# Cross-attention and a quantised feed-forward block on one core: the opening order of all five engines written anew

## The reference, cut to what matters

```
x = x + xattn(layernorm(x), ctx)      # q = x Wq, k = ctx Wk, v = ctx Wv, 8 heads of 64, softmax, Wo, bo
x = x + ffn(layernorm(x))
ffn(x) = bitlinear(silu(bitlinear(x, w_gate)) * bitlinear(x, w_up), w_down)
bitlinear(x, w) = act_quant(x) @ weight_quant(w).T
weight_quant(w): s = 1 / mean(|w|); round(w * s) clipped to -1..1, over s
act_quant(x):    s = 127 / max(|x|) per row; round(x * s), over s
```

## Time and profile before

| | before |
|---|---|
| median of 3 runs (lowest, highest) | 1103.38 us (1101.78, 1104.1) |
| profiled execution: span from first to last instruction | 1103.9 us |
| PE busy | 1079.8 us, 98% |
| DVE busy | 965.3 us, 87% |
| ACT busy | 742.6 us, 67% |
| POOL busy | 501.5 us, 45% |

### The profile page before, as it was taken

How to read it: one execution, slowest core, us unless ns; L and a number is a source line. 1 busy time by engine, 2 the same in 40 slices (tenths; PEclk the granted TensorE clock), 3 DMA queues, 4 the chain that set the end, 5 groups by cost and what they waited for, 6 DMA issues and landing times.

```text
span 1103.9 us, 17477 instructions
## 1 busy us (share of the span) xinstructions
PE 1079.8 (98%) x5528; PEld 496.4 (45%) x5528; DVE 965.3 (87%) x2081; ACT 742.6 (67%) x947; POOL 501.5 (45%) x645
## 2 busy tenths in 40 slices
PE   8879999999999999999999999999999999999998
PEld 6434444444444444444444444444444444444443
DVE  5997898998889988888989988888899889988985
ACT  3997767757656667777665677777666656666543
POOL 0255554565445454554444446555543444344111
PEclk9998999999999999999999999999999999999999
DMA  9997665353555635544564553655455555554334
GB/s 352 281 241 149 117 125 114 82 116 87 110 124 122 123 86 106 118 88 106 121 123 91 109 115 91 106 116 114 98 105 119 119 107 104 106 110 96 72 77 100
DMA packets 355963, 133.80 MB, mean 121 GB/s; under 512 B 332448, under 2 KB 332960, under 8 KB 355360
## 3 DMA queue, kind: packets, MB, share of 16 engines
q1 hardware_dynamic: 355872, 132.70, 54.4%
HBM read 34.08 MB, written 16.78 MB: 46 GB/s over the span
## 4 chain that ended last, share of the span: by engine, by line
PE 78%; DVE 7%; ACT 2%; issue 1%; DMA 1%; POOL 0%; SPq 0%; DVEq 0%; ACTq 0%; POOLq 0%
PE ps L1401 35%; PE ps L1422 18%; PE ps L1337 8%; PE ps L1340 8%; PE ps L1338 8%; DVE FF L1074 1%; DVE hm L1083 1%; PE ps L1330 1%; DVE hm L1078 1%; PE ps L1325 1%; DMA FF<-FF 1%; DVE bns L1060 1%; ACT FF L851 0%; DVE am L1128 0%; DVE xr L1066 0%
## 5 line engine op out<-in xcount | busy, mean ns | idle before, releaser
L1401 PE MATMUL ps<-wgT,FF 128*128 128x512 bf16 x1024 | 263.1, 379 | 1.6 <-ACT FF L851 1.6
L1401 PE MATMUL ps<-wW,FF 128*128 128x512 bf16 x1024 | 262.8, 379 | 0.3 <-DVE FF L1074 0.3
L1422 PE MATMUL ps<-wW,FF 128*128 128x512 bf16 x1024 | 231.5, 379 | 1.1 <-DVE xr L1066 0.9
L851 ACT ACTIVATE FF<-ps,sgu 128x512 f32<-128x512 f32 x256 | 173.1, 680 | 62.7 <-PE ps L1401 60.8
L1074 DVE TENSOR_TENSOR FF<-FF,ps 128x512 f32<-128x512 f32 x256 | 173.8, 681 | 47.2 <-ACT FF L851 26.7
L860 ACT ACTIVATE FF<-FF,c 128x1024 int16<-128x1024 f32 x128 | 141.1, 1141 | 73.8 <-DVE c L1087 73.6
L706 POOL TENSOR_TENSOR AT<-AT,rd 128x512 f32<-128x512 f32 x64 | 67.7, 1057 | 220.1 <-DVE rd L1119 216.5
L1422 PEld LDWEIGHTS ps<-wW,FF 128*128 128x128 bf16 x1024 | 99.8, 98 | 122.6 <-issue 2.1
L1401 PEld LDWEIGHTS ps<-wW,FF 128*128 128x128 bf16 x1024 | 99.7, 98 | 122.5 <-DVE FF L1074 3.8
L1401 PEld LDWEIGHTS ps<-wgT,FF 128*128 128x128 bf16 x1024 | 97.7, 98 | 123.9 <-issue 4.5
L694 POOL TENSOR_TENSOR xhl<-xn,xhl 128x512 f16<-128x512 f32 x64 | 74.3, 1161 | 85.1 <-ACT xhl L867 85.1
(11 more groups left out here) (146 smaller groups left out, 1751.9 us busy)
## 6 DMA issues: line engine op xcount, KB each, us to landing
xr<-in_x SPq DMA_DIRECT2D x64, 256.0 KB, 2.8
out<-xr SPq DMA_DIRECT2D x64, 256.0 KB, 2.3
FF<-in_L_ffn_w_gate SPq DMA_DIRECT2D x4, 1024.0 KB, 12.3
wW<-in_L_ffn_w_up SPq DMA_DIRECT2D x4, 1024.0 KB, 15.4
FF<-in_L_ffn_w_down SPq DMA_DIRECT2D x4, 1024.0 KB, 6.3
FF<-FF SPq DMA_TRANSPOSE x192, 3.3
MV<-in_L_xattn_Wq SPq DMA_DIRECT2D x1, 1024.0 KB, 8.4
MV<-in_L_xattn_Wo SPq DMA_DIRECT2D x1, 1024.0 KB, 15.7
```

The source lines that it names most:

```text
L851: eng.activation(h[:, i % 2, f * 512:(f + 1) * 512], G[n % 2][:, :], ACT.Silu, scale=sgu[:, 0, i % W:i % W + 1]).then_inc(a_si, 1)
L1401: mm = eng.matmul(bank[n % 2][:, :].rearrange("p (o f) -> p o f", o=4), qxT[:, i % 2, k, :], w[:, 4 * f:4 * f + 4, k, :], start=(k == 0), ...
L1422: mm = eng.matmul(y_bank(i)[:, :], hT[:, i % 2, c, :], wdT[:, c, :], start=(c == 0), stop=(c == 15))
```

## The change

The five strings of `OPENING` are replaced. Each holds the same names as before, in another order; no piece is added, dropped or moved to another engine, and no wait, tile or size differs. The strings are three lines shorter, so that the number of every line of code behind them is lower by three (L1337 is now L1334). Three lines of the table, before and after:

```diff
             "sync": (
-                "load_ctx, load_x 2, load_wk, load_wq, load_gate 0, load_wv, load_gate 3, load_x 0, load_gate 1, "
+                "load_x 0, load_ctx, load_x 1, load_x 2, load_wk, load_wq, load_gate 0, load_gate 1, load_wv, "
...
             "tensor": (
...
-                "14, keep 4, scores 0, keep 5, total 1, max_spread 2, max_turn 3, scores 1, keep 6, max_spread 3, "
-                "keep 7, round_X 0 4, scores 2, round_X 0 5, round_X 0 6, keep 8, round_X 0 7, scores 3, attend 0, "
...
+                "keep 4, keep 5, total 1, max_turn 2, scores 1, keep 6, max_spread 2, max_turn 3, max_spread 3, "
+                "scores 2, keep 7, round_X 0 4, keep 8, round_X 0 5, round_X 0 6, round_X 0 7, scores 3, attend 0, "
```

More of the change, by code:

```diff
@@ L398, in xattn_ffn @@
             "sync": (
-                "load_ctx, load_x 2, load_wk, load_wq, load_gate 0, load_wv, load_gate 3, load_x 0, load_gate 1, "
-                "load_x 1, load_gate 2, load_up 0, load_up 1, load_wo, load_bo, load_up 3, load_x 3, load_up 2, "
[17 rows of a table removed]
-            "gpsimd": (
[18 rows of a table removed]
-            "scalar": (
[30 rows of a table removed]
-            "vector": (
[38 rows of a table removed]
+                "load_x 0, load_ctx, load_x 1, load_x 2, load_wk, load_wq, load_gate 0, load_gate 1, load_wv, "
+                "load_gate 3, load_x 3, load_up 0, load_gate 2, turn_x 0, load_up 1, load_wo, load_up 2, load_bo, "
[16 rows of a table added]
+            "gpsimd": (
[18 rows of a table added]
+            "scalar": (
[29 rows of a table added]
+            "vector": (
[37 rows of a table added]
             "tensor": (
                 "keep 0, setup 0, setup 1, setup 2, keep 1, setup 3, setup 4, max_turn 0, setup 5, max_spread 0, "
[20 rows of a table removed]
[20 rows of a table added]
         }
```

## The result

| | before | after |
|---|---|---|
| median of 20 runs (lowest, highest) | 1103.56 us (1099.5, 1105.98) | 1099.38 us (1098.39, 1103.11) |
| ratio to before | | 0.9976, 95% interval 0.9965 to 0.9988 |
| profiled execution: span, granted clock | 1103.9 us, 0.993 | 1097.4 us, 0.998 |

The change makes the kernel faster by 0.24%, 2.6 us by the ratio, with the interval from 1.3 to 3.9. (The medians are 4.2 us apart, because before has runs near 1100 and near 1104 and its median jumps between them; the means are 2.6 apart, as the ratio says.) The forecast was 7.3 us less than the profiled execution of before. From one profiled span to the other it is indeed 6.5 us, and that is the trap of this case: the spans differ by far more than the kernels do.

A forecast was written before the change was run, and what follows sets the result against it. PE was taken as the bound, busy 1079.8 of 1103.9 us; 8.0 lead + 2.3 behind - 3 disturbance = 7.3 us off the span, 1096.6, less 0.5 gives 1096.1 us. Range for 8 in 10: 1090.5 to 1104.

The forecast's parts named there:

- Sum: Whole kernel: 8.0 + 2.3 - 3 = 7.3 us off the profiled span of 1103.9, median 0.5 below span: 1096.1 us.
- lead up to `gate_up 0 0`: Opening: the first `gate_up` starts at 88.5 us instead of 96.51, a lead of 8.0 us.
- Behind it: After `gate_up 0 0`: waits of 0.99 and 2.19 us go, new ones of 0.9 come, plus 2.3 us.
- Disturbance: DVE instructions lengthened beside POOL's: 3 us taken off the gain, with 0 and 6 as ends.
- Loads, `mean 0`: Opening: reordered loads on SP cost nothing; `mean 0` on DVE starts at 33.0 us instead of 35.1.
- `s_max 0`: DVE in the opening: `s_max 0` starts 3.5 us earlier, at 46.3 instead of 49.8 us.
- `scores 2` ahead of the long filler: PE: `scores 2` runs from 54.0 to 56.6, `round_X 0 4` starts at 63.1 instead of 64.99 us, without the 2.47 wait.
- `total 2`: PE: `total 2` at 75.3 instead of 82.98 us, 7.7 us earlier, behind a new wait of 2.0 us.
- Rival 2: From the first `gate_up` on, DVE gives back half to all of the lead: 1100 to 1104 us; 17%.
- The case in which each of the eight `clip`s of matrices 0 and 1 grows by 1 us: DVE `clip`s each meeting a POOL instruction: the lead shrinks by 8, not 3, to about 1101 us.
- Rival 1: Nothing disturbs, no low clock and no excess on DVE: 11.5 us gained, 1092 us or less; 9%.
- Rival 3: Opening: transposes of x among the loads land late and hold ACT for 9.4 us, about 1107 us; 15%.

The follow-up runs named there:

- e1: The kernel before, run again without an edit: median 1101.58 us, ratio 0.9994 to before, profiled span 1098.4 us at clock 0.998.
- e4: The changed kernel with `x_hi 2` moved on ACT from ahead of `evac 13` to behind `evac 14`: 1100.15 us, ratio 0.9967 to before.
- e17: The changed kernel with `x_hi 2` moved behind `evac 14` on ACT, the same edit as e4 on another chip: 1099.66 us, ratio 0.9971 to before.
- e8: The changed kernel with `scores 2` put back behind the long filler (`keep 7`): 1106.78 us, ratio 1.0036 to before.
- e2: The changed kernel, run again without an edit: median 1100.77 us, ratio 0.9976 to before, profiled span 1099.6 us.
- e15: The changed kernel, run once more without an edit on another chip: 1100.63 us, ratio 0.9981 to before.
- e9: Changed lists up to `gate_up 0 0`, the remaining items in the order of the kernel before: 1106.99 us, ratio 1.0033 to before.
- e10: Order of the kernel before up to `gate_up 0 0`, the remaining items in the changed order: 1107.14 us, ratio 1.0027 to before.
- e5: The kernel before with dummy matmuls in three waits of PE (5, 20 and 24 more): 1103.41 us, ratio 1.0001 to before.

## Why the prediction was wrong

The sign and the range (1090.5 to 1104) held, the size didn't: 7.3 us forecast, 2.6 measured. The main step that failed is the one called **Sum**: "The profiled span is 1103.9, so 1096.6; the median is 0.5 below the span, so 1096.1." The times are 1.7 to 1.9 us above their spans, not 0.5 below. The profiled execution of before was thus 1.8 us above the median of its 148 runs (1105.7 against 1103.9), in its slowest fifth, and everything I took from it carried its low clock. Of the 3.3 us between 1096.1 and 1099.38, 2.3 are this wrong distance from span to time; the spans themselves are 1096.6 forecast and 1097.4 measured.

That the two spans are so close is luck, for two terms missed in opposite directions. The lead up to `gate_up 0 0` was 5.2 us, not 8.0; **Behind it** and **Disturbance** together, 2.3 - 3 = -0.7 in the forecast, were +1.3.

I had also read the low stretches as the price of the waits, by their length: 2.47 us was followed by one and 2.19 wasn't, so I charged 1.7 us for a wait of 2.0. The traces don't bear that out. Before's own first stretch followed a wait of 1.72 us; in the trace after the wait of 1.85 had none behind it and that of 1.39 had; in e1 the wait of 3.02 had none, where in the profiled execution of before that of 2.95 had 6.8 us. In e1 3.4 us of low clock lie ahead of 100 us, not 13.6. By e1's base the 6.5 us between the spans shrink to 1.0 (1098.4 to 1097.4); but e1's profiled execution (1100.24 us) is itself among the fastest tenth of before's, as 11 of the 148 are as fast. At the clock of 0.998 the runs are 2.0 apart, by the ratio 2.6. Executions at 0.995 or less are rarer with the change (3 runs of 44, 46 of 148 before).

The ends of **Sum** are off a little too: 1.7 and 3 us either way of 1096.1 give 1091.4 to 1100.8, not 1092 to 1100.5.

Point by point, against the trace after:

- *Loads, `mean 0`*: 32.9 for 33.0. Right, though by e1's base (34.3) it gains 1.4, not 2.1.
- *`s_max 0`*: forecast 46.3, measured 48.42, 2.1 late. From 20 to 40 us DVE was idle for 2.5 us where I had left 0.7, the most of it (1.44) ahead of `clip 0 0` for ACT's `tern 0 0` (L839), and it waited 0.98 us more ahead of `max_v` for ACT's L758. ACT itself stood for DMAs: 0.63 us at `x_hi 1`, 0.97 at an `abs_sum` of w_up and 1.20 at `x_hi 2`. e4 and e17 took out the last alone and left `s_max 0` where it was. Which of the others sets it stays open.
- *`scores 2` ahead of the long filler*: the order is as forecast and e8 shows its worth within the new lists (6.6 us), but `scores 2` ran from 56.39 to 60.5, at the low clock, and not from 54.0 to 56.6; `round_X 0 4` is at 66.98, not 63.1. Against 64.99 before it is later, though `scores 2` is then done.
- *`total 2`*: 79.02 behind 1.85, forecast 75.3 behind 2.0. The new wait was right, the time 3.7 late; all of the lead that is missing at `gate_up 0 0` was missing here. Lead 4.0 against the profiled execution, 2.7 against e1.
- *`gate_up 0 0`*: forecast 88.5, measured 91.31. The lead of 8.0 is 5.2 against that execution and 1.0 against e1 (92.27); in e2 (92.99) and e15 (92.08) it is -0.7 and 0.2 against e1. The way from `total 2` was forecast well, 13.2 us against 12.3 measured, with PE and `turn_q 0` arriving together as I had said.
- *Behind it*: the forecast was 2.3. The wait of 2.19 us for tile 7 is gone and PE is idle for 1.65 us from 100 to 140, in waits of up to 0.79. From 91 us to the end the lead grows by 1.3 against the profiled execution (5.2 to 6.5) and not at all against e1. Rival 2 (DVE gives the lead back) did not happen: from 100 to 200 us PE is idle for 2.05 us in all, with no wait for `mult` over 1 us.
- *Disturbance*: the 3 us were a cut for DVE's long instructions. No run separated it. The case in which each of the eight `clip`s of matrices 0 and 1 grows by 1 us did not arise: in the trace after they take 0.68 to 0.70 us each. Long ones stand elsewhere (`copy_x 0` with 0.98 us, a `clip` of matrix 2 with 1.64).

Rival 1 fell. Rival 3's sign came, at a fifth of its size: `turn_x 0` was issued at 25.7 us and landed 5.1 us later, just past the 30.7 at which it was to decide, `turn_x 1` took 9.9 us to land, and ACT stood for 0.63 and 1.20 us, not for 9.4; the time is not above the old one. A rival was missing: that the profiled execution is one of the slower ones and more than half of the 6.5 us is its own. The clock of 0.83 in one stretch of the earlier trace rows and the missing time around the span were the place to ask.

What stays open: where the 2.6 us of the runs come from. The traces at like clock (e1 against after, e2 and e15) hardly show them, and e9 and e10 broke at the seam, so that what lies ahead of `gate_up 0 0` and behind it can't be told apart.

## What to carry to other kernels

Before a saving is priced from one profiled execution, ask which of the kernel's executions it is: compare its mean granted clock and its time, span and what lies around it, with the other runs, and price low stretches as a chance, not as a fixed cost of a wait. When one engine's list is cleared on the way to a transfer, read the list of the engine that issues the transfer too: the hold moves to whatever stands ahead there. And lists of several engines that were ordered together are one unit: here each half of the new order, joined to the rest of the old one, was worse than either whole.

## What the runs showed of the hardware

- The same wait of TensorE is followed by low clock in one execution and not in the next: 2.95 us with 6.8 us at half clock behind it in the profiled execution of before, 3.02 us with none in e1.
- With the low clock gone in 11 of 12 runs (e5, which has 49 dummy matmuls more), the times still spread from 1102.05 to 1105.83 and their median stood 3.3 us above that of the kernel before at a clock of 0.999 or 1.0 (1103.4 against 1100.1).
- Issuing the same transpose took SP 1.23 us in e1 and 2.58 in e5, at the same place in the list and 0.2 us apart in time.
